# Rewritten first attention stage, early attention weights, late weights and a three-pass last stage in a program of eight stages

## The chip, the core and the metric

The program runs on one NeuronCore of one Trainium2 chip. The metric is the device time of one execution in microseconds (us), the median over the runs shown. PE is TensorE, ACT is ScalarE, DVE is VectorE, POOL is GpSimd and SP is SyncE, which here only issues DMAs. PSUM is the memory that PE writes its products to, in eight banks of 512 f32 columns; SBUF is the memory of the weights and the activations.

## What is computed

The input x is (8, 256, 256) in f32: eight items of 256 rows and 256 features. Eight stages follow each other, and each ends with the same step, x = layernorm(x + stage(x)):

- l0a: RMS norm, a projection to 1284 columns (gate 512, input 512, step 4, B and C 128 each), a causal convolution of 4 taps, SiLU, and a Mamba-2 scan with 4 heads and a state of 128
- l0f: gated MLP of 1024 with int8 weights
- l1a: attention with 16 heads of 128 (weights 256 x 6144 and 2048 x 256)
- l1f: mixture of 32 experts, 4 for each row
- l2a: Mamba-1 scan; l2f: gated MLP with ternary weights
- l3a: a transformer block with one key/value head, causal, and an MLP of 1024
- l3f: gated MLP of 688 with a shared LoRA and 8 LoRA experts of rank 8, 2 for each row

The heart of l0a, and l3f, cut to what matters:

```python
h = x * rsqrt(mean(x * x) + 1e-6) * norm_scale
proj = h @ in_proj_w                      # gate | ssm_in | dt_raw | B | C
ssm_in = silu(conv4(ssm_in) + conv_bias)
dt = softplus(dt_raw + dt_bias);  A = -exp(A_log)
cum = cumsum(A * dt)                      # within chunks; chained over them
y = (exp(cum_i - cum_j) * (C_i . B_j) * dt_j, only j <= i) @ x_h
y = (y + D * ssm_in) * silu(gate)
stage = x + y @ out_proj_w
```

```python
scores = sigmoid(x @ W_router); pick 2 of scores + expert_bias
gate = x @ W_gate + lora(x, sA_gate, sB_gate) + expert_lora(x, A_gate, B_gate, w)
up   = x @ W_up + ...                     # the same form
hidden = silu(gate) * up
out  = hidden @ W_down + ...              # the same form, on hidden
```

## The kernel before

The list `PHASES` holds one function for each stage, and the program calls them one after the other. x stays in SBUF throughout (`sh.X`). Each stage is a block with its own buffers, its own semaphores and one hand-written instruction stream for each engine; at its end all engines meet in a barrier. Nothing of a stage starts in the one before it. Within a stage all engines loop over the eight items, two per pass of a hardware loop (`Fori`); an item is two tiles of 128 rows. The order within an engine is the order of the code, and waits on semaphore counts tie the engines together. There is no planner.

**Before l0a** a first block loads all eight items of x.

**l0a.** SP loads eight small arrays, then the input weights wi and the output weights wo (L240 to L247), and PE's first projection (`project_in`, L293) waits for both. For each item: DVE scales the input rows (`scaled`, L463), PE turns them (L104), ACT keeps the result as xT (L112). `project_in` gives the input columns and the raw steps; DVE convolves (`convolve`, L479 and L481, 16 instructions), ACT takes SiLU (L395), PE turns the rows back. The decays are summed over runs and chunks (`sum_decays`), PE spreads the running sums over all partitions (cum) and turns the shares (L349); `share` is copied by DVE. Then come 16 instructions of DVE that add the share and the causal mask `hide` to the sums (ld, L589), the exponentials on ACT (lt, L433, L437, L441: two whole tiles of 512 columns and eight of 64), the products with CB and dt on DVE (mt, L599), the product with x on PE (yv), and on DVE yu (L608) and the gated yg (L613). PE turns yg and multiplies with wo (L380) into the bank Y. `add_and_stats` (L135) and `normalize` (L163) on DVE, with the square root between them on POOL (`rstd`, L156), end the item. The gates are projected into the same banks as the sums (W[4], W[5]), so they come first in an item and ACT takes their SiLU before the sums are written.

**l0f, l1a: three passes.** Here a product of two f32 matrices is three products of fp32r matrices (`product`, L787 and the lines behind it): high x high, low x high and high x low. ACT copies a matrix into its high half, DVE subtracts it from the original and leaves the low half. l0f's items have nine steps; DVE forms a (L759) and al, the low half of an earlier step's a (L765), and ACT the high half ah (L731). The down projection of an item (`down`, L684) waits for all eight al. In l1a SP loads the weights in 16 pieces into three slots; ACT casts (L966) and DVE subtracts (L1022) all 16 ahead of the first item, in their code, and PE waits for four pieces before every fourth head of the first item.

**l3a, l3f.** Each loads its weights at its own start (L2555 and following; L3072 and following). In l3a POOL makes wkr, a copy of the key weights (L2589), ahead of PE's first query product (L2629). l3f works in plain f32: per item five chunks of 128 hidden columns and one of 48, each with six products into one of three banks GU (L3119, L3120), the down projection with 24 instructions over 328 columns (L3131), then the LoRA end (haw turned, L3137 and L3141). `route` (L3180 to L3199) picks the experts on DVE, for the next item, behind the fourth chunk.

## Time and profile before

| | |
|---|---|
| Median of 3 runs (lowest, highest) | 2817.87 us (2817.5, 2819.13) |
| Profiled execution, its own time | 2824.52 us |
| Its span | 2822.8 us |
| PE busy (share) | 2324.8 us (82%) |
| DVE busy | 1728.7 us (61%) |
| ACT busy | 1424.7 us (50%) |
| POOL busy | 787.0 us (28%) |
| Granted clock of PE, mean | 0.902 of 2.4 GHz |

The stages stand in the span at: l0a 10.4 to 321.8 us, l0f to 455.2, l1a to about 1000, l1f to about 1540, l2a to 1988.5, l2f to 2143.4, l3a to 2555, l3f to 2814.1. Busy times are shares of the whole span, in which stages with different limits stand side by side; so windows by stage are read first, then the timeline of the engines within a stage. In a timeline a row gives the start, the duration, engine, line, operation, destination and sources, and in brackets how long the engine was idle before it and what released it; a row with xN stands for N instructions in succession.

### The profile page before, as it was taken

How to read it: one execution, taken by the hardware profiler on the slowest of the kernel's cores; microseconds unless marked ns; L12 is line 12 of the kernel's file. 1: busy time of each engine (PE TensorE's matmuls, PEld its weight loads, DVE VectorE, ACT ScalarE, POOL GpSimd, SP SyncE). 2: the span in 40 equal slices, each digit the busy share in tenths (PEclk: the TensorE clock that was granted, in tenths of full speed). 3: DMA queues.
4: the chain of work that ended last, by engine and by line, in shares of the span. 5: the costliest groups of instructions: out<-in, count | busy, mean ns of one | idle time of the engine just before them, and what ended most of it. 6: DMA issues, size and time to landing. Idle time of an engine off the chain costs nothing. (4 is left out here: it accounts for less than half of the span.)

```text
span 2822.8 us, 47695 instructions
## 1 busy us (share of the span) xinstructions
PE 2324.8 (82%) x15564; PEld 1976.3 (70%) x15564; DVE 1728.7 (61%) x4180; ACT 1424.7 (50%) x3573; POOL 787.0 (28%) x795
## 2 busy tenths in 40 slices
PE   4888783999999953999658888998685899895997
PEld 3666683999999952999536666777684567674765
DVE  4777575788888834554248888778463575641332
ACT  3444443777777711333267666775332665651222
POOL 1111010000000044000247787778483122220000
PEclk8777897999999956999879999999896999997999
DMA  4000003000000084333311111100001000001000
GB/s 123 0 0 0 14 0 119 1 2 2 3 2 3 2 247 135 116 117 102 115 57 46 46 46 46 57 35 1 23 0 42 1 1 0 0 0 43 0 0 30
DMA packets 77709, 111.40 MB, mean 39 GB/s; under 512 B 15162, under 2 KB 64050, under 8 KB 76484
## 3 DMA queue, kind: packets, MB, share of 16 engines
q1 hardware_dynamic: 70020, 87.36, 9.8%
q0 software_dynamic: 7488, 21.50, 2.4%
q8 instruction: 109, 1.79, 0.3%
q14 instruction: 92, 0.75, 0.1%
HBM read 79.86 MB, written 28.97 MB: 39 GB/s over the span
## 5 line engine op out<-in xcount | busy, mean ns | idle before, releaser
L1756 POOL TENSOR_TENSOR l2a_hb<-l2a_hb,l2a_Cb 128x1024 f32<-128x1024 f32 x128 | 303.2, 2380 | 112.8 <-DVE l2a_hb L2212 111.8
L2212 DVE TENSOR_TENSOR_SCAN l2a_hb<-l2a_dA,l2a_dB 128x1024 f32<-128x1024 f32 x128 | 288.4, 2274 | 63.0 <-PE l2a_dB L1837 30.1
L2066 ACT ACTIVATE l2a_dA<-l2a_delta,l2a_An 128x255 f32<-128x255 f32 x512 | 214.4, 497 | 37.2 <-DVE l2a_delta L2152 20.9
L1837 PE MATMUL l2a_dB<-l2a_diag,l2a_dxT 64*128 64x128 f32 x2048 | 190.9, 308 | 31.1 <-DVE l2a_hb L2212 18.3
L1837 PEld LDWEIGHTS l2a_dB<-l2a_diag,l2a_dxT 64*128 64x128 f32 x2048 | 141.5, 196 | 95.4 <-PE l2a_dB L1837 37.5
L793 PE MATMUL l1a_QK<-l1a_xh,l1a_wqkv_h 128*128 128x256 f32 x512 | 146.7, 286 | 13.7 <-DVE l1a_wo L1022 10.4
L793 PE MATMUL l1a_QK<-l1a_xh,l1a_wqkv 128*128 128x256 f32 x512 | 145.6, 284 | 0.0
L793 PE MATMUL l1a_QK<-l1a_xl,l1a_wqkv_h 128*128 128x256 f32 x512 | 145.4, 284 | 0.0
L1857 PE MATMUL l2a_YS<-ident,l2a_hb 128*128 128x128 f32 x1024 | 143.3, 287 | 1.0 <-POOL l2a_hb L1756 1.0
L1001 ACT ACTIVATE l1a_ex<-l1a_S,l1a_nm 128x256 f32<-128x256 f32 x256 | 119.2, 471 | 36.9 <-DVE l1a_nm L1053 36.9
L1857 PEld LDWEIGHTS l2a_YS<-ident,l2a_hb 128*128 128x128 f32 x1024 | 117.4, 146 | 12.4 <-issue 1.7
L2848 ACT ACTIVATE l3a_ex<-l3a_sm,l3a_nm 128x128 f32<-128x128 f32 (+1 forms) x256 | 99.0, 448 | 50.8 <-DVE l3a_nm L2985 50.2
L1036 DVE TENSOR_TENSOR l1a_qkl<-l1a_QK,l1a_qkh 128x512 fp32r<-128x512 f32 x128 | 88.2, 690 | 50.5 <-ACT l1a_qkh L976 37.1
L154 POOL TENSOR_TENSOR l1a_vpe<-l1a_mv,eps 128x2 f32<-128x2 f32 x8 | 1.6, 197 | 413.3 <-DVE l1a_mv L148 413.3
L1563 DVE TENSOR_TENSOR l1f_a<-l1f_s,l1f_GU 128x96 f32<-128x96 f32 x95 | 24.1, 254 | 143.3 <-ACT l1f_s L1417 143.3
L793 PEld LDWEIGHTS l1a_QK<-l1a_xh,l1a_wqkv_h 128*128 128x128 f32 x512 | 98.2, 192 | 14.4 <-issue 14.4
L2979 DVE TENSOR_TENSOR l3a_sm<-l3a_S,l3a_hide 128x512 f32<-128x512 f32 x96 | 65.7, 684 | 54.7 <-PE l3a_S L2698 54.7
L793 PEld LDWEIGHTS l1a_QK<-l1a_xl,l1a_wqkv_h 128*128 128x128 f32 x512 | 98.4, 192 | 0.0
L1353 PE MATMUL l1f_GU<-l1f_wS,l1f_xt 128*128 x380 | 98.3, 382 | 0.0
L793 PEld LDWEIGHTS l1a_QK<-l1a_xh,l1a_wqkv 128*128 128x128 f32 x512 | 98.3, 192 | 0.0
L976 ACT CAST l1a_qkh<-l1a_QK 128x512 fp32r<-128x512 f32 x128 | 75.6, 592 | 32.7 <-PE l1a_QK L793 32.4
L793 PE MATMUL l1a_S<-l1a_qkh 128*128 128x256 f32 x256 | 73.2, 286 | 22.4 <-DVE l1a_qkl L1036 22.2
(577 smaller groups left out, 7281.6 us busy)
## 6 DMA issues: line engine op xcount, KB each, us to landing
l2a_Cb<-c_rows SPq DMA_DIRECT2D x8, 2048.0 KB
l1f_xl<-moe_x_rows SPq DMA_DIRECT2D x95, 128.0 KB, 2.0
moe_y_rows<-l1f_yo SPq DMA_DIRECT2D x95, 128.0 KB, 1.7
l1a_raw<-in_L_attn_w_qkv_dram SPq DMA_DIRECT2D x12, 512.0 KB, 4.6
moe_x_rows<-X SPq DMA_DIRECT2D x1, 4224.0 KB, 17.3
l1f_dL<-in_L_ffn_Wd_dram SPq DMA_DIRECT2D x1, 3072.0 KB
X<-in_L_attn_x_dram SPq DMA_DIRECT2D x8, 256.0 KB, 4.6
l1a_raw<-in_L_attn_w_o_dram SPq DMA_DIRECT2D x4, 512.0 KB, 4.3
```

The source lines that it names most:

```text
L793: ins = pe.matmul(out, a, b, start=(first and n == 0), stop=(last and n == len(passes) - 1), **more)
L976: nc.scalar.copy(qkh[:, h % 2].rearrange("p n t -> p (n t)"), QK[h % 2][:, :]).then_inc(qk_kept, 1)
L1001: last = nc.scalar.activation(ex[:, h % 2, j, :], S[h % 2][:, j * SEQ:(j + 1) * SEQ], ACT.Exp, bias=nm[:, h % 2, j:j + 1], scale=SCALE, ac ...
L1036: nc.vector.tensor_tensor(qkl[:, h % 2].rearrange("p n t -> p (n t)"), QK[h % 2][:, :], qkh[:, h % 2].rearrange("p n t -> p (n t)").bitcas ...
L1353: last = nc.tensor.matmul(GU[t % 2][:, 2 * EI:2 * (EI + SI)], xt[t % 2][:, kc, :], wS[:, kc, bass.ds(small, 1), :], start=(kc == 0), stop= ...
L1756: nc.gpsimd.tensor_tensor(h[:, :, :], h[:, :, :], Cb[p][:, s0:s0 + UN, :], ALU.mult).then_inc(hc_ready, 1)
L1837: last = nc.tensor.matmul(out[:, m:m + 2, j * P + a:j * P + a + HP], dxT[q][a:a + HP, j, c * P:(c + 1) * P], diag[q][a:a + HP, j, s0 + m:s ...
L1857: last = nc.tensor.matmul(YS[j][:, c * P:(c + 1) * P], hb[u % RING][:, n, j * P:(j + 1) * P], sh.ident[:, :], is_transpose=True, start=Fal ...
L2066: last = nc.scalar.activation(dA[(i * NU + u) % DAS][:, n, 1:SEQ], delta[q][:, c, 1:SEQ], ACT.Exp, scale=An[:, c, s0 + n:s0 + n + 1])
L2212: nc.vector.tensor_tensor_scan(flat(hb[u % RING]), flat(dA[(i * NU + u) % DAS]), dB[u % 2][:, :], 0.0, ALU.mult, ALU.add).then_inc(scanned, 1)
L2848: last = nc.scalar.activation(ex[:, b % NB, cols], sm[:, b % NB, cols], ACT.Exp, bias=nm[:, b % NB, n:n + 1])
L2979: nc.vector.tensor_tensor(m, S[b % 3][:, :].rearrange("p (h k) -> p h k", h=nh), hide[:, None, 2 * P - keys_n:2 * P].to_broadcast([P, nh, ...
```

## The change

It has five parts.

1. **Loads at the start.** Only item 0 of x is loaded ahead of l0a. The other seven are issued in l0a by SP, behind wi and six of its small arrays, and before wo. The norm scale is loaded as two columns for each partition and applied by ACT when it keeps xT.
2. **l0a is rewritten.** The mask is added on PE: a bf16 identity times four copies of the mask, accumulated onto the sums in PSUM. ACT takes all exponentials straight from PSUM, 24 of 64 columns, with the share as bias; ld and its DVE instructions are gone. The gates go to the banks T and Y, late in an item. The projections, the convolution (now in two halves) and the decay sums of the next item are placed between the parts of the present one; what belongs to item i+1 or i+2 is left out in the last items by `left`. Items 0, 1, 6 and 7 are written out, 2 to 5 loop. The scaling of the input moves from DVE to ACT.
3. **Early weights.** l1a's wqkv is loaded, cast and subtracted in l0f, in 24 pieces of 512 columns, four in each of items 2 to 7. l1a itself keeps four pieces of wo, in steps 3 to 6 of its first item.
4. **Late weights.** The loads of l3a (23 DMAs) and l3f (21) are issued in l2f, behind its own, into buffers that stay until the end.
5. **l3f in three passes.** Weights, inputs, hidden tile and LoRA halves are split into high and low, and PE uses `product`. The end of an item (haw, LoRA, residual, normalisation) is moved behind the first chunks of the next.

The loads at the start, in SP's code of l0a:

```diff
-            sp.dma_start(nsb[:, :], row(w["L0_attn_norm_scale"])).then_inc(small_loaded, 16)
-            sp.dma_start(cw[:, :, :], w["L0_attn_conv_weight"]).then_inc(small_loaded, 16)
-            sp.dma_start(cb[:, :], w["L0_attn_conv_bias"]).then_inc(small_loaded, 16)
+            sp.dma_start(ns[:, :], w["L0_attn_norm_scale"]).then_inc(ns_loaded, 16)
+            sp.dma_start(wi[:, :, :], w["L0_attn_in_proj_w"].rearrange("(k p) n -> p k n", p=P)).then_inc(w_loaded, 16)
...
+            sp.dma_start(cw[:, :, :], w["L0_attn_conv_weight"]).then_inc(small_loaded, 16)
+            sp.dma_start(cb[:, :], w["L0_attn_conv_bias"]).then_inc(small_loaded, 16)
+            for b in range(1, ITEMS):
+                sp.dma_start(sh.X[:, b], sh.x_dram[:, b]).then_inc(sh.x_rest, 16)
             sp.dma_start(Db[:, :], row(w["L0_attn_D"])).then_inc(small_loaded, 16)
-            sp.dma_start(wi[:, :, :], w["L0_attn_in_proj_w"].rearrange("(k p) n -> p k n", p=P)).then_inc(w_loaded, 16)
             sp.dma_start(wo[:, :, :], w["L0_attn_out_proj_w"].rearrange("(k p) n -> p k n", p=P)).then_inc(w_loaded, 16)
```

PE in one item of l0a (after the inputs are turned), and the mask:

```diff
                 last.then_inc(la_turned, 1)
 
+            def mask(j):
+
+                return nc.tensor.matmul(W[4 + j][:, :], identb[:, :], hide4[:, :, :].rearrange("p h t -> p (h t)"),
+                                        start=False, stop=True, skip_group_check=True)
+
+            def decays(k):
+
+                pe.wait_ge(yT_kept, k * NT)
+                pe.wait_ge(cumR_ready, (k + 1) * 2)
+                for j in (1, 0):
+                    for h in range(NH):
+                        last = nc.tensor.matmul(W[4 + j][:, h * P:(h + 1) * P], sel[:, h, :], cumR[:, j * P:(j + 1) * P],
+                                                start=(h == 0), stop=(h == NH - 1), skip_group_check=True)
+                    if j == 0:
+                        last = mask(0)
+                    last.then_inc(cum_ready, 1)
+                pe.wait_ge(share_ready, k + 1)
+                for n in range(len(SHARES)):
+                    last = nc.tensor.matmul(W[3][:, SEQ + n * NH:SEQ + (n + 1) * NH], shareR[:, n, :], ph.ident[0:NH, 0:NH],
+                                            start=True, stop=True)
+                last.then_inc(share_turned, 1)
...
+                if left:
+                    steps_in(i + 1, 1 - p)
+                    pe.wait_ge(xtm_ready, (i + 1) * NT)
+                    ssm_in(i + 1, 1 - p, 0)
+                pe.wait_ge(lt_ready, i * 3 + 1)
+                mask(1).then_inc(mask_ready, 1)
+                if left:
+                    ssm_in(i + 1, 1 - p, 1)
+                pe.wait_ge(ph.y_added, i)
+                for j, bank in enumerate((ph.T, ph.Y)):
+                    for kc in range(KC):
+                        last = nc.tensor.matmul(bank[:, :], ph.xT[p][:, kc, j * P:(j + 1) * P], wi[:, kc, 0:DI],
+                                                start=(kc == 0), stop=(kc == KC - 1))
+                    last.then_inc(gate_ready, 1)
+                pe.wait_ge(xtm_ready, (i + 1) * NT)
```

ACT's exponentials in an item of l0a:

```diff
+                    nc.scalar.copy(xtm[p][:, j, :], W[j][:, :]).then_inc(xtm_ready, 1)
+                act.wait_ge(m_ready, i * 3)
+                act.wait_ge(share_kept, i + 1)
+                act.wait_ge(cum_ready, (i + 1) * NT)
+                for n in ORDER:
+                    s, t = BLOCKS[n]
+                    if n == 2:
+                        act.wait_ge(mask_ready, i + 1)
                     for h in range(NH):
                         for u in range(NT):
-                            last = nc.scalar.activation(lt[:, 1, h, u * CHUNK:(u + 1) * CHUNK],
-                                                        W[5][:, h * P + u * CHUNK:h * P + (u + 1) * CHUNK], ACT.Exp,
-                                                        bias=share[:, SHARES.index((0, NT + u)), h:h + 1])
+                            cols = slice(u * CHUNK, (u + 1) * CHUNK)
+                            m = SHARES.index((s, NT * t + u))
+                            last = nc.scalar.activation(lt[:, n, h, cols], W[4 + t][:, h * P + u * CHUNK:h * P + (u + 1) * CHUNK],
+                                                        ACT.Exp, bias=share[:, m, h:h + 1])
                     last.then_inc(lt_ready, 1)
-                    nc.scalar.activation(lt[:, 2], ld[:, 1], ACT.Exp).then_inc(lt_ready, 1)
+                if left:
```

DVE in the same item:

```diff
+                    steps.begin(i + 1)
+                    dt_magnitude(i + 1)
+                dve.wait_ge(cb_ready, i + 1)
+                dve.wait_ge(yv_ready, i * NT)
+                for done, n in enumerate(ORDER):
+                    s, t = BLOCKS[n]
+                    dve.wait_ge(lt_ready, i * 3 + done + 1)
+                    for h in range(NH):
+                        last = nc.vector.scalar_tensor_tensor(out=mt[:, n, h, :], in0=W[2][:, n * P:(n + 1) * P],
+                                                              scalar=dt[:, s, h:h + 1], in1=lt[:, n, h, :],
+                                                              op0=ALU.mult, op1=ALU.mult)
+                    last.then_inc(m_ready, 1)
+                if left:
+                    one_plus(i + 1)
+                    convolve(i + 1, (0, 1))
+                for j in range(NT):
```

The early pieces in l0f, on SP, ACT and DVE, and those that stay in l1a, on DVE:

```diff
+            for m in range(PIECES):
+                if m >= SLOTS:
+                    sp.wait_ge(early.low_ready, m - SLOTS + 1)
+                kc, c = m // (PIECES // KC), m % (PIECES // KC) * 512
+                sp.dma_start(raw[m % SLOTS][:, :].bitcast(F32), early.src[:, kc, c:c + 512]).then_inc(qkv_loaded[m % SLOTS], 16)
...
+                    if 4 <= step < 4 + SLOTS and split:
+                        act.wait_ge(qkv_loaded[step - 4], (i - 1) * 16)
+                        nc.scalar.copy(high[:, i * 4 - 8 + step - 4, :], raw[step - 4][:, :].bitcast(F32)).then_inc(early.high_ready, 1)
...
+                    if 5 <= step < 5 + SLOTS and split:
+                        n = i * 4 - 8 + step - 5
+                        dve.wait_ge(early.high_ready, n + 1)
+                        nc.vector.tensor_tensor(low[:, n, :], raw[step - 5][:, :].bitcast(F32), high[:, n, :].bitcast(F32),
+                                                ALU.subtract).then_inc(early.low_ready, 1)
...
+                        dve.wait_ge(w_high, step - 2)
+                        _, came, high, low = piece(step - 3)
+                        nc.vector.tensor_tensor(low, came, high.bitcast(F32), ALU.subtract).then_inc(w_low, 1)
```

The late loads, in l2f:

```diff
+            sh.late.load_l3_attn(sp)
+            sh.late.load_l3_ffn(sp)
```

l3f: a chunk and the down projection on PE, the hidden tile's high half on ACT and low half on DVE:

```diff
+                    for half, wh, wl, bh, bl in ((0, wgh, wgl, bgh, bgl), (1, wuh, wul, buh, bul)):
+                        parts = [(wh[:, kc, cols], wl[:, kc, cols], xh[p][:, kc, :], xl[p][:, kc, :]) for kc in range(KC)]
+                        parts += [(bh[:, cols], bl[:, cols], xawh[:, p, half, :], xawl[:, p, half, :])]
+                        last = product(nc.tensor, GU[n % 3][0:rows, half * SEQ:(half + 1) * SEQ], parts)
...
+                        router_and_a(pe, i + 1, 1 - p)
+                pe.wait_ge(ph.y_added, i * NT)
+                if first:
+                    pe.wait_ge(w_low, 6)
+                for j in range(NT):
+                    tile = slice(j * P, (j + 1) * P)
+                    for f, rows in CH:
+                        if j == 0:
+                            pe.wait_ge(hid_low, i * FC + f + 1)
+                        if j == 0 and f == FC - 1:
+                            turn_xaw(pe, i + 1)
+                        last = product(nc.tensor, YB[j][:, 0:D + LR],
+                                       [(hh[0:rows, f, tile], hl[0:rows, f, tile], wdh[0:rows, f, :], wdl[0:rows, f, :])],
+                                       first=(f == 0), last=(f == FC - 1))
...
+                        act.wait_ge(gu_used, i * FC + f + 1)
+                        if f == 0:
+                            act.wait_ge(down_ready, i * NT)
+                        nc.scalar.copy(hh[0:rows, f, :], hid[0:rows, n % 3, :]).then_inc(hid_high, 1)
...
+                        dve.wait_ge(hid_high, i * FC + f + 1)
+                        nc.vector.tensor_tensor(hl[0:rows, f, :], hid[0:rows, n % 3, :], hh[0:rows, f, :].bitcast(F32), ALU.subtract
+                                                ).then_inc(hid_low, 1)
```

How the change moves instructions is shown at three places. The first is ACT in l0a, in the order of the code before: xT is kept, then the exponentials of the decays (lt, from the tiles ld and from the bank W) and the SiLU of the next item's convolution (xs from cv).

```order
L112 COPY l0a_xT<-l0a_T 128x512
L431 REGISTER_ALU
L433 ACT_TABLE_LOAD
L433 ACTIVATE l0a_lt<-l0a_ld 128x512
L437 ACTIVATE l0a_lt<-l0a_W,l0a_share 128x64 x8
L441 ACTIVATE l0a_lt<-l0a_ld 128x512
L392 REGISTER_ALU
L394 ISA
L395 ACT_TABLE_LOAD
L395 ACTIVATE l0a_xs<-l0a_cv,l0a_cb 128x256
```

With the change, from keeping xT to the end of the gates (sg):

```order
L456 ACTIVATE l0a_xT<-l0a_T,l0a_ns 128x256 x2
L489 COPY l0a_xtm<-l0a_W 128x512 x2
L501 ACT_TABLE_LOAD
L501 ACTIVATE l0a_lt<-l0a_W,l0a_share 128x64 x24
L470 ACTIVATE l0a_e<-l0a_ax 128x8
L474 ACT_TABLE_LOAD
L474 ACTIVATE l0a_ln<-l0a_w 128x8
L510 ACT_TABLE_LOAD
L510 ACTIVATE l0a_sg<-l0a_T 128x512
L510 ACTIVATE l0a_sg<-l0a_Y 128x512
```

The exponentials are 24 small instructions now, all from PSUM; the exponential of the step (e) follows them directly, and the gates' SiLU stands behind them and not ahead.

The second place is DVE in the loop of l0f, before: a, its low half al, and the normalisation of the item before (L163).

```order
L759 SCALAR_TENSOR_TENSOR l0f_a<-l0f_GU,l0f_su,l0f_gs 128x256
L765 TENSOR_TENSOR l0f_al<-l0f_a,l0f_ah 128x256
L756 REGISTER_ALU
L759 SCALAR_TENSOR_TENSOR l0f_a<-l0f_GU,l0f_su,l0f_gs 128x256
L765 TENSOR_TENSOR l0f_al<-l0f_a,l0f_ah 128x256
L163 TENSOR_SCALAR X<-l0f_r,l0f_mv,l0f_rstd 128x256
```

And with the change:

```order
L862 SCALAR_TENSOR_TENSOR l0f_a<-l0f_GU,l0f_su,l0f_gs 128x256
L868 TENSOR_TENSOR l0f_al<-l0f_a,l0f_ah 128x256
L878 ISA
L879 ISA
L879 TENSOR_TENSOR early_wqkv<-l0f_raw,early_wqkv_h 128x512
L859 REGISTER_ALU
L862 SCALAR_TENSOR_TENSOR l0f_a<-l0f_GU,l0f_su,l0f_gs 128x256
L868 TENSOR_TENSOR l0f_al<-l0f_a,l0f_ah 128x256
L163 TENSOR_SCALAR X<-l0f_r,l0f_mv,l0f_rstd 128x256
```

A difference of 128x512 elements stands behind al in each of the steps 5 to 8 of an item.

The third is PE in l3f, the first product of a chunk, before:

```order
L3119 MATMUL l3f_GU<-l3f_xT,l3f_wg 128x256 x2
L3120 MATMUL l3f_GU<-l3f_xawT,l3f_bg 128x256
L3119 MATMUL l3f_GU<-l3f_xT,l3f_wu 128x256 x2
L3120 MATMUL l3f_GU<-l3f_xawT,l3f_bu 128x256
L3119 MATMUL l3f_GU<-l3f_xT,l3f_wg 128x256 x2
```

With the change, the half of a chunk that makes the gate:

```order
L901 MATMUL l3f_GU<-l3f_xh,l3f_wgh 128x256
L901 MATMUL l3f_GU<-l3f_xl,l3f_wgh 128x256
L901 MATMUL l3f_GU<-l3f_xh,l3f_wgl 128x256
L901 MATMUL l3f_GU<-l3f_xh,l3f_wgh 128x256
L901 MATMUL l3f_GU<-l3f_xl,l3f_wgh 128x256
L901 MATMUL l3f_GU<-l3f_xh,l3f_wgl 128x256
L901 MATMUL l3f_GU<-l3f_xawh,l3f_bgh 128x256
L901 MATMUL l3f_GU<-l3f_xawl,l3f_bgh 128x256
L901 MATMUL l3f_GU<-l3f_xawh,l3f_bgl 128x256
```

Each f32 product has become three.

## Rows read from the trace of the kernel before

**Rows 1.** Windows: us, busy (count) of PE, PEld, DVE, ACT, POOL; clock, DMA, GB/s

```profile
10.40:321.80 311.40, 232.94 (x1126) 192.57 (x1126) 208.94 (x680) 141.61 (x282) 36.36 (x49) 0.80 0.07 21
455.20:512.00 56.80, 21.92 (x140) 20.93 (x140) 30.66 (x44) 29.35 (x49) 1.68 (x4) 0.64 0.47 148
512.00:1000.00 488.00, 478.60 (x3994) 476.77 (x3992) 396.80 (x1071) 375.74 (x1129) 12.36 (x23) 1.00 0.01 2
1988.50:2143.40 154.90, 117.83 (x884) 113.68 (x884) 87.61 (x220) 53.56 (x143) 104.65 (x158) 0.87 0.03 11
2555.00:2814.10 259.10, 219.25 (x960) 161.75 (x960) 70.89 (x325) 59.65 (x104) 12.31 (x27) 0.93 0.05 12
```

**Rows 2.** Timeline of the start: start, us, engine, line, operation, count, [idle before <-releaser]

```profile
14.68 0.47 SPq L247 DMA_DIRECT2D l0a_wo<-n_L_attn_out_proj_w_dram  x1
...
23.82 0.79 PE L293 MATMUL l0a_W<-l0a_xT,l0a_wi 128*128 128x256 f32 x1 [2.47 <-DMA l0a_wo<-n_L_attn_out_proj_w_dram]
```

**Rows 3.** Timeline of one item of l0a

```profile
152.20 2.77 DVE L463 SCALAR_TENSOR_TENSOR l0a_xin<-X,l0a_inv,l0a_nsb 128x256 f32<-128x256 f32 x2 [0.92 <-POOL l0a_inv L255]
...
158.06 1.28 ACT L433 ACT_TABLE_LOAD   x1 [0.38 <-DVE l0a_ld L589]
...
159.89 1.73 ACT L437 ACTIVATE l0a_lt<-l0a_W,l0a_share 128x64 f32<-128x64 f32 x8
...
160.01 1.12 DVE L599 SCALAR_TENSOR_TENSOR l0a_mt<-l0a_W,l0a_dt,l0a_lt 128x128 f32<-128x128 f32 x4 [0.50 <-ACT l0a_lt L433]
...
165.41 5.02 DVE L481 SCALAR_TENSOR_TENSOR l0a_cv<-l0a_W,l0a_cw,l0a_cv 128x255 f32<-128x255 f32 x12
...
181.61 0.69 DVE L135 SCALAR_TENSOR_TENSOR l0a_r<-X,l0a_Y 128x512 f32<-128x512 f32 x1 [2.01 <-PE l0a_Y L380]
...
184.44 0.74 DVE L163 TENSOR_SCALAR X<-l0a_r,l0a_mv,l0a_rstd 128x256 f32 x2 [1.08 <-POOL l0a_rstd L156]
```

**Rows 4.** Line L613: count, min/median/max ns, first and last start

```profile
L613 DVE TENSOR_TENSOR l0a_yg<-l0a_yu,l0a_sg x16: 680/681/685, 69.5 to 308.9; 128x512 f32<-128x512 f32 x16
```

**Rows 5.** Window of l0f's steady part, and DVE's timeline in it

```profile
340.00:440.00 100.00, 90.05 (x725) 86.20 (x724) 71.96 (x187) 49.87 (x125) 11.78 (x18) 1.00 0.00 1
...
357.72 1.02 DVE L163 TENSOR_SCALAR X<-l0f_r,l0f_mv,l0f_rstd 128x256 f32<-128x256 f32 x2
...
394.67 0.68 DVE L126 TENSOR_TENSOR l0f_xl<-l0f_T,l0f_xh 128x512 fp32r<-128x512 f32 x1
...
442.67 0.73 DVE L163 TENSOR_SCALAR X<-l0f_r,l0f_mv,l0f_rstd 128x256 f32 x2
```

**Rows 6.** Timeline of l1a's start, ACT, DVE and PE

```profile
459.02 0.69 DVE L126 TENSOR_TENSOR l1a_xl<-l1a_T,l1a_xh 128x512 fp32r<-128x512 f32 x1 [3.95 <-ACT l1a_xh L119]
...
460.11 1.04 ACT L966 CAST l1a_wqkv_h<-l1a_raw 128x1024 fp32r<-128x1024 f32 x1 [1.12 <-DMA l1a_raw<-in_L_attn_w_qkv_dram]
...
461.18 1.23 DVE L1022 TENSOR_TENSOR l1a_wqkv<-l1a_raw,l1a_wqkv_h 128x1024 fp32r<-128x1024 f32 x1 [1.47 <-ACT l1a_wqkv_h L966]
...
495.97 0.58 PE L793 MATMUL l1a_S<-l1a_qkh 128*128 128x256 f32 x1 [22.23 <-DVE l1a_qkl L1036]
```

**Rows 7.** Timeline of l3a's start, the first query matmuls on PE

```profile
2164.71 1.62 PE L2629 MATMUL l3a_T<-l3a_xT,l3a_wq 128*128 128x256 f32 x3 [16.23 <-POOL l3a_wkr L2589]
```

**Rows 8.** Timeline of PE in l3f, and a window of 40 us in l1a

```profile
2581.98 2.07 PE L3119 MATMUL l3f_GU<-l3f_xT,l3f_wg 128*128 128x256 f32 x4 [0.75 <-ACT l3f_xawT L3152]
...
2640.52 1.03 PE L3119 MATMUL l3f_GU<-l3f_xT,l3f_wg 128*128 128x256 f32 x4
...
2641.39 0.60 PE L3120 MATMUL l3f_GU<-l3f_xawT,l3f_bg 72*128 72x256 f32 x2
...
2658.86 7.47 PE L3131 MATMUL l3f_Y<-l3f_wd,l3f_hid 128*128 128x328 f32 x24 [0.99 <-DVE l3f_hid L3217]
...
2668.80 1.03 PE L3119 MATMUL l3f_GU<-l3f_xT,l3f_wg 128*128 128x256 f32 x4
...
520.00:560.00 40.00, 40.00 (x338) 40.00 (x337) 32.04 (x85) 31.98 (x96) 0.84 (x1) 1.00 0.01 2
```

848 lines of the change are left out of this document (484 added, 364 removed).

## The prediction

> **What bounds the kernel now.** I read the busy time by stage first. The change touches the stages l0a (first attention), l0f, l1a, the start of l2f, l3a and l3f [rows 1]. TensorE (PE) is the busiest engine in each, but only l1a behind its first 57 us is solid: 478.60 us busy in 488.00. In l0a PE is busy for 232.94 of 311.40 us and is granted a clock of 0.80 on average (1 is 2.4 GHz, 0.50 is 1.2 GHz); l1a's first part has 21.92 busy in 56.80.
>
> Then the timeline, for what ends PE's waits. At the start the output weights are issued at 14.68 us, behind the input weights, and the first projection runs at 23.82, released by them [rows 2]. In l0a the reader is to see a serial chain over DVE, ACT and PE [rows 3, 4]. In l1a PE's second group of work starts at 495.97 after 22.23 us of waiting, behind casts of 1.04 us (ACT) and differences of 1.23 us (DVE) that turn the weights into two halves [rows 6]. l3a waits 16.23 us for weights [rows 7], and l3f starts only at 2581.98 and then runs in f32 at about 0.216 us per instruction, two instructions per product [rows 8].
>
> **The change, part by part.** Its own time is 2824.52 us for a span of 2822.8; the median of the runs is 2817.87. I take the difference of spans off the median.
>
> *Start and l0a.* Only one of eight input tiles is loaded ahead of the stage; seven move behind the projection weights, but the output weights stand behind all of these, and PE waits for both. Behind the stage's start, which comes some 7 us earlier, the loads carry 4.0 MB instead of 2.2. I put the first projection at 19 us; bounds are 17 (all moves at the rate of a full queue) and 24 (as now). From 19 on: projections at the low clock and two taps of the convolution 9.7; dt, la and the sums 4.7; the other taps 3.4; silu, staging, turn and copies 4.8, which is 41.6; from the table load to the first gated product 12.8 as in the cycle below, and 0.8 for slow matmuls: 55.2. That product (L613) now starts at 69.5 [rows 4]: 14.3 less.
>
> A cycle runs from one item's gated products to the next; there are two an item, 0.6 apart, so it is (308.9-69.5-0.6)/7 = 34.1 us [rows 4]. The new one, at PE's full clock: DVE forms dt and la (0.95), PE turns la (0.65), DVE sums (2.9), convolves two taps (8 of the 12 instructions of 5.02 us: 3.35), then 0.2, and the residual chain from 181.61 to 185.18 (3.57) [rows 3], and copies the shares (0.25): 11.9. ACT loads its table (1.28) and takes 24 exponentials at 1.73/8 = 0.216: 5.2, with gaps 6.65. This makes 18.55. DVE multiplies the last block (1.12), forms 1+e (0.4), convolves two taps (3.3), and adds and gates (1.28 each): 26.2 with a few gaps. Gone from it are DVE's 16 additions of mask and share, each of 64 columns, now two bf16 matmuls of 512 columns on PE, for which no row stands (twice fp32r's 0.118 for 256 columns is 0.24 each [rows 8]), two table loads, and the scaled input on DVE, 2.77 us beside POOL's product [rows 3]. The later stages of PE, behind the share copy, are 11.2 us of matmuls, and reach the same point as DVE, 23.7 against 23.5: no slack. A clock of 0.9 adds 1.2 us. I take 27.5. The bounds are 26.2, and 31, which is 29.1 us (232.94/8) of PE busy time as now plus 2 of waits. Six cycles give 6 x 6.6 = 39.6. The last cycle has no next item to prepare: 24.5 against 34.1, 9.6 less. The tail, from the last gated pair to the stage's end at 321.7, falls from 13.4 to 8.1, since the sums for a next item no longer stand in it: 5.3. Sum **-68.8**.
>
> *l0f.* Items 2 to 7 take four pieces of the l1a weights each, a cast on ACT and a two-input difference of 128x512 on DVE. DVE is busy for 71.96 of 100 us and ACT for 49.87 [rows 5], so by averages it all fits. But the down projection waits for DVE's last difference (al), and three of the four new ones stand ahead of it in DVE's queue. An instruction of this size takes 0.68 [rows 5]: 6 items x 3 x 0.69 = 12.4, and I take **+13**; the bounds are 0 (hidden by the waits that DVE has) and 20 (4 each, and PE's clock falling once an item). The pair of normalisations takes 1.02 us beside POOL's copy of an input tile and 0.73 in the item where there is none [rows 5]. The Trainium skill (SBUF — State Buffer, Who interferes with whom) says that a DVE instruction with two SBUF inputs and a GpSimd instruction that reads SBUF exclude each other for a whole instruction; by it each item might lose another POOL copy's length, and the term would be nearer to its upper bound. That speaks against the pieces being placed here.
>
> *l1a.* Weights are ready, so the first group of S products can follow at 464 us instead of 495.97: the input's low half is ready at 459.7, two halves of QK at the 1.2 GHz level take 2.5, the split 1.2. Four pieces of wo stay, in the first item's steps 3 to 6, 1.04 and 1.23 each beside a DVE that is 80% busy (396.80 of 488.00): they cost 1.5 [rows 1, 6]. **-30.5**, bounds -24 (the pieces delay their full length) and -33.
>
> *l2f.* 44 loads are issued behind the three that its start waits for. **+0.5**, bounds 0 and 4 (they share the engines with these three). The issue time itself, 44 x 0.47 = 21 us, lies beside 150 us of the stage.
>
> *l3a.* PE has turned the input when its 16.23 us of waiting begin, at 2148.5 [rows 7]; ACT keeps it in 1 us more, POOL's copy of the key weights (0.4) is done before that, so the first query matmul runs at 2149.7 instead of 2164.71: **-15**, bounds -13 and -16.
>
> *l3f.* Weights are there; ACT and DVE split four of them first, 4.2 and 5.0 us by the elements of [rows 6], behind the routing: start at 2570.7, 11.3 less. An f32 product of 256 columns costs two instructions of 0.216; three fp32r passes cost 3 x 0.118, as 40 us of l1a hold 338 of them [rows 8]. So GU falls from 15.5 to 12.7 us an item. The down projection has 328 columns: now 24 instructions in 7.47 us; 36 passes of 0.118 x 328/256 = 0.15 make 5.4 (bounds 4.9 and 6.2: the f32 form needs 10% over its share). With turns, router and the LoRA end PE has 20.9 us. The LoRA end of an item is moved behind the next item's first chunk, so that chain leaves the path, but a new one enters: scores wait for ACT behind chunk 3, routing takes 3.3 us of DVE, and the fifth and sixth differences come behind it, while PE stands at the down projection. I get 2.6 us of waits: 23.5 an item, against 28.3 (2668.80-2640.52, [rows 8]). Eight items with 3.5 of slow clock at first: 191.5, against 228.3 now (2640.52-2581.98 for the first two, and six more). The tail is 2 longer. **-46.1**, bounds -34 and -54.
>
> Sum: -68.8+13-30.5+0.5-15-46.1 = -146.9. 2817.87-146.9 = **2671**.
>
> **The rivals.** *The clock follows the small waits.* The two rewritten stages wait briefly and often. l2f does so with 117.83 busy in 154.90 and is granted 0.87; but l0f's steady part runs at 1.00 and l3f at 0.93, its start included [rows 1, 5]. With l2f's clock, 20.9 becomes 24.0 in l3f, +25 us; in l0a the cycle goes to 29.6, +15: 2711. The Trainium skill (TensorE: Matmul & The Clock Gate, A second HAM failure mode: psum-queue depth-cycling) has it that short, frequent idling between matmul groups that cycle through PSUM banks makes the clock oscillate; l3f's three banks would fit that, and the granted 1.00 of l0f's steady part, which cycles through four, speaks against it [rows 5].
>
> *DVE and ACT set l3f's cycle.* The hidden tile now needs six casts and six differences more and two hand-overs per chunk. If the routing chain costs 7 us and not 2.6, the item is back at 28 us and only the start is gained: 2671+36 = 2707. For it speaks that the order of each engine is fixed; against, that DVE is busy for 70.89 of 259.10 us there now [rows 1].
>
> *The loads don't hide.* Early pieces late, or l2f's first loads slowed: 2690.
>
> *Slower.* In both rewritten stages PE's clock stays at the 1.2 GHz level throughout. Then l0a's 22.4 us of matmuls become 45 a cycle, +76-14 = +62, and l3f's items 42, +110-9 = +101; with l0f +13 and -45.5 from l1a and l3a this gives 2949. It decides once the mean clock of both falls below some 0.62; l0a now has 0.80 with longer waits than I expect, which speaks against it.
>
> **How the numbers follow.** Forecast 0.75, clock rival 0.12, l3f's cycle 0.08, loads 0.03, slower 0.02. The first has its own range from its bounds, added as independent: 2650 to 2695. To keep 8 in 10 with the two rivals near 2710, the range is 2645 to 2712. A measurement here tells 0.2% (5.6 us) from no change; only the last case is on the other side, and 0.01 is left to no change: faster 0.97, same 0.01, slower 0.02.
>
> **What would show it.** In the trace of the changed kernel: first projection near 19 us; gated products 27.5 us apart; l0f's items 16.3 us apart instead of 14.2 ((442.67-357.72)/6, [rows 5]), with PE waiting for al; l1a's first S product 8 us behind its start; no DMA wait in l3a; fp32r at 0.118 in l3f, a wait of some 1.6 us in the down projection, 23.5 us an item, clock 0.9 or more. An l0a clock under 0.8, or an l3f item over 26, would make the prediction wrong.

## The result, and the profile after

The changed kernel takes 2675.48 us (median of 4 runs, 2671.42 to 2687.0) against 2818.5 us for the kernel before (4 runs): the ratio is 0.9493, with an interval of 0.9466 to 0.9521. That is 143.0 us less; 146.9 less was forecast, and 2671. The profiled execution is the longest of the four, 2687.0 us of its own time for a span of 2685.3; what follows is read from it. Further down, one run of the kernel before (3229.18 us, at a granted clock of 0.713) is a slow one and left out of its median and its ratios.

The page of the changed kernel, busy time by engine, and PE's granted clock in 40 slices:

```profile
PE 2271.4 (85%) x15926; PEld 1964.0 (73%) x15926; DVE 1702.8 (63%) x4081; ACT 1443.0 (54%) x3765; POOL 781.0 (29%) x796
...
PEclk9888999999999758999779989999797999998999
```

PE is busy for 53.4 us less than before and the span is 137.5 us shorter, so most of the gain is waiting that is gone. A stage is taken here from the end of the last normalisation (L163) of the stage before to the end of its own last one:

| stage, us | before | after | difference | forecast |
|---|---|---|---|---|
| start and l0a | 321.7 | 258.5 | -63.2 | -68.8 |
| l0f | 133.4 | 141.8 | +8.4 | +13 |
| l1a | 544.8 | 508.5 | -36.3 | -30.5 |
| l1f to l2f | 1143.4 | 1150.4 | +7.0 | +0.5 |
| l3a | 411.6 | 397.2 | -14.4 | -15 |
| l3f | 258.9 | 219.7 | -39.2 | -46.1 |

The +7.0 is no effect of the change. 6.5 of it lie in the expert loop of l1f, which the change does not touch: from its first to its last matmul it took 264.8 us before and 271.3 here. Among the twelve experiments below, all with this loop, eleven take 264.8 to 266.1 and one 273.0 (`g_three`), and the stretch from l1f to l2f takes 1129.4 to 1144.2 us. So the loop takes one of two lengths with the same code; why is open. It may also be what sets the profiled execution 11 us above the median; the other runs have no trace that would show it.

Windows of the changed kernel (us, busy and count of PE, PEld, DVE, ACT and POOL; clock, DMA share, GB/s): l0a's steady part, l0f's, the start of l1a, l2f, and l3f:

```profile
100.00:208.00 108.00, 103.98 (x545) 85.50 (x545) 75.20 (x248) 68.10 (x199) 14.31 (x20) 0.88 0.00 1
300.00:380.00 80.00, 66.13 (x534) 63.07 (x533) 61.48 (x157) 43.82 (x108) 8.44 (x15) 1.00 0.22 66
400.50:457.30 56.80, 48.90 (x371) 46.99 (x372) 38.88 (x92) 39.01 (x107) 2.28 (x5) 0.91 0.12 38
1905.00:2059.00 154.00, 116.59 (x884) 112.07 (x884) 87.66 (x224) 53.52 (x143) 105.06 (x159) 0.88 0.17 49
2456.00:2676.00 220.00, 191.47 (x1344) 176.30 (x1344) 101.96 (x399) 81.29 (x164) 12.33 (x27) 0.93 0.00 1
```

l0a's steady part has become one in which PE is busy for 96% of the time. Before, the steady part had 82%, in the next line (75% in [rows 1] is with the start):

```profile
100.00:300.00 200.00, 163.13 (x798) 135.68 (x799) 143.11 (x470) 98.77 (x198) 25.27 (x30) 0.80 0.00 0
```

l1a's first 57 us hold 48.90 us of PE where they held 21.92; l2f, with 17% of DMA beside it, is as long as it was. l0f went the other way: 83% of PE where it had 90% [rows 5].

The two gated products an item in l0a (count, min/median/max ns, first and last start), to be set beside [rows 4]:

```profile
L674 DVE TENSOR_TENSOR l0a_yg<-l0a_yu,l0a_sg x16: 681/683/686, 58.3 to 249.7; 128x512 f32<-128x512 f32 x16
```

A cycle is (249.7-58.3-0.6)/7 = 27.3 us.

The timeline of the changed kernel at the places that the forecast named (start, duration, engine, line, operation, idle before it and releaser):

```profile
21.44 1.87 PE L311 MATMUL l0a_W<-l0a_wi,l0a_xT 128*128 128x4 f32 x8 [11.52 <-DMA l0a_wo<-n_L_attn_out_proj_w_dram]
...
174.87 1.86 PE L365 MATMUL l0a_W<-ident,l0a_shareR 4*128 4x4 f32 x12
...
222.48 1.28 DVE L674 TENSOR_TENSOR l0a_yg<-l0a_yu,l0a_sg 128x512 f32<-128x512 f32 x2
...
249.10 1.28 DVE L674 TENSOR_TENSOR l0a_yg<-l0a_yu,l0a_sg 128x512 f32<-128x512 f32 x2
...
337.38 0.69 DVE L133 TENSOR_TENSOR l0f_r<-X,l0f_ys 128x512 f32<-128x512 f32 x1
...
344.24 0.38 PE L784 MATMUL l0f_Y<-l0f_wd,l0f_ah 128*128 128x256 f32 x1 [1.59 <-DVE l0f_al L868]
...
352.61 0.69 DVE L133 TENSOR_TENSOR l0f_r<-X,l0f_ys 128x512 f32<-128x512 f32 x1
...
405.08 0.55 PE L901 MATMUL l1a_QK<-l1a_xh,early_wqkv_h 128*128 128x256 f32 x1 [1.49 <-DVE l1a_xl L126]
...
409.38 0.39 PE L901 MATMUL l1a_S<-l1a_qkh 128*128 128x256 f32 x1
...
2065.64 1.62 PE L2712 MATMUL l3a_T<-l3a_xT,late_wq 128*128 128x256 f32 x3 [1.27 <-ACT l3a_xT L2890]
...
2473.34 0.55 PE L901 MATMUL l3f_GU<-l3f_xh,l3f_wgh 128*128 128x256 f32 x1 [4.19 <-DVE l3f_xawl L3341]
...
2542.53 0.52 DVE L3329 TENSOR_TENSOR l3f_xaw<-l3f_LX,l3f_wf 128x144 f32<-128x144 f32 x2
...
2543.31 0.41 DVE L3367 TENSOR_TENSOR l3f_hl<-l3f_hid,l3f_hh 128x256 fp32r<-128x256 f32 x1
...
2543.78 0.42 PE L901 MATMUL l3f_Y<-l3f_wdh,l3f_hh 128*128 128x328 f32 x1 [1.32 <-DVE l3f_hl L3367]
...
2545.61 0.60 PE L3176 MATMUL l3f_XT<-ident,l3f_xaw 128*72 128x128 f32 x4 [0.46 <-DVE l3f_hl L3367]
```

What is to be seen, in order of time. The first projection is still released by the output weights, which stand behind seven input tiles now; PE has waited 11.52 us for them. In l0f an item is 352.61-337.38 = 15.23 us long (14.15 before, from [rows 5]), and the down projection waits for al, as the forecast had it. Over five items PE's wait for al is 1.62 us in the mean, against 0.19 before. l1a's first S product starts at 409.38, 9.1 us behind the stage's start at 400.3; it had been 40.9. l3a has no DMA wait left: the query product waits only for its input, 6.4 us behind the start at 2059.2 (21.4 before). And in l3f the low half hl, on which the down projection waits, comes right behind the end of the routing chain (L3329) in DVE's order.

### The profile page after: what moved, and what is told of

Its sections match the earlier page's. It is cut to its first block and busy times, and to the rows that moved or that the text cites. A ratio compares the mean times of both kernels' runs of the same rounds, so it can differ in the third digit from the quotient of the medians.

```text
span 2685.3 us, 48369 instructions
## 1 busy us (share of the span) xinstructions
PE 2271.4 (85%) x15926; PEld 1964.0 (73%) x15926; DVE 1702.8 (63%) x4081; ACT 1443.0 (54%) x3765; POOL 781.0 (29%) x796
## 5 line engine op out<-in xcount | busy, mean ns | idle before, releaser
L2314 DVE TENSOR_TENSOR_SCAN l2a_hb<-l2a_dA,l2a_dB 128x1024 f32<-128x1024 f32 x128 | 288.4, 2275 | 62.5 <-PE l2a_dB L1939 28.8
L2168 ACT ACTIVATE l2a_dA<-l2a_delta,l2a_An 128x255 f32<-128x255 f32 x512 | 214.3, 497 | 37.5 <-DVE l2a_delta L2254 20.9
L1939 PEld LDWEIGHTS l2a_dB<-l2a_diag,l2a_dxT 64*128 64x128 f32 x2048 | 141.8, 197 | 96.3 <-PE l2a_dB L1939 37.8
L901 PE MATMUL l1a_QK<-l1a_xh,early_wqkv_h 128*128 128x256 f32 x512 | 144.2, 282 | 5.1 <-issue 3.6
L901 PE MATMUL l1a_QK<-l1a_xl,early_wqkv_h 128*128 128x256 f32 x512 | 143.2, 280 | 0.0
L901 PE MATMUL l1a_QK<-l1a_xh,early_wqkv 128*128 128x256 f32 x512 | 143.1, 280 | 0.0
L1665 DVE TENSOR_TENSOR l1f_a<-l1f_s,l1f_GU 128x96 f32<-128x96 f32 x95 | 24.1, 254 | 140.0 <-ACT l1f_s L1519 140.0
L901 PEld LDWEIGHTS l1a_QK<-l1a_xh,early_wqkv_h 128*128 128x128 f32 x512 | 97.3, 190 | 5.9 <-issue 5.9
L901 PEld LDWEIGHTS l1a_QK<-l1a_xl,early_wqkv_h 128*128 128x128 f32 x512 | 97.2, 190 | 0.0
L901 PEld LDWEIGHTS l1a_QK<-l1a_xh,early_wqkv 128*128 128x128 f32 x512 | 97.1, 190 | 0.0
L2938 ACT COPY l3a_eT<-l3a_PT 128x512 f32<-128x512 f32 x96 | 55.4, 577 | 70.9 <-PE l3a_PT L2827 70.8
L1091 ACT ACTIVATE l1a_pr<-l1a_ex,l1a_rz 128x256 f32<-128x256 f32 x128 | 65.3, 510 | 44.0 <-DVE l1a_rz L1142 40.4
```

The source lines that it names most:

```text
L901: ins = pe.matmul(out, a, b, start=(first and n == 0), stop=(last and n == len(passes) - 1), **more)
L1091: nc.scalar.activation(pr0[:, h % 2, :], ex[:, h % 2, 0, :], ACT.Copy, scale=rz[:, h % 2, 0:1]).then_inc(probs_ready, 1)
L1939: last = nc.tensor.matmul(out[:, m:m + 2, j * P + a:j * P + a + HP], dxT[q][a:a + HP, j, c * P:(c + 1) * P], diag[q][a:a + HP, j, s0 + m:s ...
L2168: last = nc.scalar.activation(dA[(i * NU + u) % DAS][:, n, 1:SEQ], delta[q][:, c, 1:SEQ], ACT.Exp, scale=An[:, c, s0 + n:s0 + n + 1])
L2314: nc.vector.tensor_tensor_scan(flat(hb[u % RING]), flat(dA[(i * NU + u) % DAS]), dB[u % 2][:, :], 0.0, ALU.mult, ALU.add).then_inc(scanned, 1)
```

## The experiments

The first four kernels undo one part each; they ran on one chip, where the kernel before took 2813.09 us (7 runs). The change itself did not run beside these or the later kernels. Its 2675 us go with 1150.4 us from l1f to l2f, and these four take 1129.4 to 1135.2 there; so their totals come out below the expected ones, and the reading goes by stage. A stage with unchanged code is not the same in every profile either: l0a takes 255.0 to 258.5 us, l3f 216.5 to 222.9.

### The old l0a

The stage and its first loads are those of before; the rest is changed.

```diff
-            for b in range(1, ITEMS):
-                sp.dma_start(sh.X[:, b], sh.x_dram[:, b]).then_inc(sh.x_rest, 16)
...
-                mask(1).then_inc(mask_ready, 1)
...
+                    nc.scalar.activation(lt[:, 0], ld[:, 0], ACT.Exp).then_inc(lt_ready, 1)
```

> The changed kernel with the first attention stage and the first loads of before (all eight input tiles ahead of the stage). Parts add up: l0a ends at 321.7 us again and not at 258.5, nothing behind it moves, 2675 + 63 = 2739 us. Parts depend on each other (the early pieces or the stage behind profit from what l0a leaves, a clock or a queue): the other stages change their length and the sum is off by more than 5 us from 2739.

Measured: 2726.89 us, ratio 0.970 (0.9678 to 0.9722). l0a is back at 320.4 us, +61.9 against the change, and l0f, l1a, l3a and l3f stay within 1.6 us of it. The total is 12 us below the expected 2739, which by its own words speaks for parts that depend on each other. But the stretch from l1f to l2f, at 1131.3 us, is 19 us shorter than in the change's profile, and it is as short (1129.4 to 1135.2) in the three kernels beside it that keep the new l0a. So the stages do not lean on each other, and the terms can be read one by one.

### The old weights of l1a

l0f has no pieces, and l1a loads and splits all 16 of its own.

```diff
-                    item(it * 2 + p, p, split=True)
+                    item(it * 2 + p, p)
...
+            for m in range(len(PIECES)):
+                dve.wait_ge(w_high, m + 1)
+                _, came, high, low = piece(m)
+                nc.vector.tensor_tensor(low, came, high.bitcast(F32), ALU.subtract).then_inc(w_low, 1)
```

> The changed kernel with l0f and l1a of before: all 16 weight pieces are split in front of l1a's first item. If the pieces cost l0f their displacement of al and the missing split is l1a's whole gain: l0f's items go from 15.27 back to 14.1-14.2 us, the stage from 141.8 to 133-134, l1a from 508.5 to 545; 2675 + 28 = 2703 us. Rival: l0f is longer for another reason (its start behind the new l0a); then it stays above 140 us and the time is 2711.

Measured: 2701.33 us, ratio 0.9594 (0.9566 to 0.9622). l0f takes 134.0 us (-7.8), l1a 547.9 (+39.4). The part is worth 31.6 us by its stages and would be worth 39 if l0f paid nothing. l0f's items are back at 14.1 us, so the new l0a ahead of it is not what made them longer.

### The late loads in their own stages

The same DMAs, issued at the start of l3a and of l3f.

```diff
-            sh.late.load_l3_attn(sp)
-            sh.late.load_l3_ffn(sp)
...
+        @block.sync
+        def _(sp):
+            sh.late.load_l3_attn(sp)
```

> The changed kernel with the 23 and 21 late loads issued at the starts of l3a and l3f themselves. If they are hidden in l2f: l2f keeps 154 us; l3a gets its wait of about 14.5 us back; in l3f the router product runs 19 us behind the stage's start instead of 4.2, 15 us more; 2675 + 29 = 2704 us. Rival: the 44 loads and their buffers cost something in l1f, l2a or l2f (the three were 7 us longer in the profile of the change): then these three return to 1143 us together and the time is 2697.

Measured: 2686.21 us, ratio 0.9548 (0.9522 to 0.9574). l3a is some 11 us longer than this change's in the other kernels (408.3 against 396.6 to 397.6), l3f 13.0 longer (232.7 against 219.7), both somewhat less than expected, and l1f to l2f take 1129.4 us against 1129.7, 1131.3 and 1135.2 in its neighbours on the chip: the 44 transfers cost l2f nothing that can be seen.

### l3f in f32

The changed l3f with its order and its early weights, but one f32 product where there are three of fp32r. The low halves are formed and not used.

```diff
-        xh, xl = ([ph.sb(f"{n}{q}", [P, KC, SEQ], F32R) for q in range(2)] for n in ("xh", "xl"))
+        xh, xl = ([ph.sb(f"{n}{q}", [P, KC, SEQ], F32) for q in range(2)] for n in ("xh", "xl"))
...
-                        last = product(nc.tensor, GU[n % 3][0:rows, half * SEQ:(half + 1) * SEQ], parts)
+                        last = single(nc.tensor, GU[n % 3][0:rows, half * SEQ:(half + 1) * SEQ], parts)
```

> The changed kernel with l3f in its new order but in f32: one f32 product where three fp32r ones stand; the casts and differences stay (the low halves are then zero and no product reads them). If the gain is in PE's passes: an item goes from 24.3 to 27.5-29 us (GU +2.8, down +2.1, less a wait of 1.5), 2675 + 26 to 38, about 2707 us. Rival: the new order of the item is what gained: the item stays under 26 us and the time under 2689.

Measured: 2682.95 us, ratio 0.9537 (0.9514 to 0.9561); l3f takes 236.0 us, +16.3. Its window of 140 us:

```profile
2500.00:2640.00 140.00, 138.94 (x615) 101.90 (x614) 57.78 (x234) 44.99 (x96) 7.22 (x15) 1.00 0.00 0
```

And the same window of the changed kernel:

```profile
2500.00:2640.00 140.00, 131.44 (x943) 122.50 (x941) 64.87 (x268) 51.60 (x111) 8.65 (x18) 0.96 0.00 1
```

In f32 PE is busy for 99% of it and an item takes 26.6 us; with three passes PE is busy for 94% and an item takes 24.1 to 24.35 (one took 28.4, at a lower granted clock). So the shorter products free more of PE than the stage gets. The outcome lies between the two expectations: an item is shorter than the 27.5 to 29 us of the first and longer than the 26 of its rival, since the new order is worth something too. With one f32 product, PE's busy time in an item is as before (26.5 us against 26.6), and its waits fall from 1.66 us to 0.1: from 28.3 to 26.6 an item, 13 us in eight. Of the whole 39.2 us of l3f, then, 13.0 are the loads and 16.3 the three passes; 9.9 are left for the order less what the splitting at the start costs, and these two were not taken apart.

### Four parts moved alone

These ran together on another chip (kernel before 2812.22 us, 3 runs), two runs each. The first brings l3f's routing forward by a step, behind the second chunk, and sets the residual behind it:

```diff
-                    if step == 2 and not first:
-                        residual(i - 1)
-                    if step == 3:
+                    if step == 2:
                         route(dve, i + 1, 1 - p)
+                    if step == 3 and not first:
+                        residual(i - 1)
```

> The changed kernel; in l3f router, scores and routing of the next item come one chunk earlier (router behind chunk 1, scores and routing in step 2, the residual in step 3). If the down projection waits because the routing stands ahead of the last differences on DVE: its waits (2.4 us an item) go to under 0.5, PE's clock rises above 0.96, an item takes 21.5-22.3 us instead of 24.3 and l3f 199-206 us instead of 219.7. Rival: the wait only moves (chunk 3's hidden tile now waits for the routing): an item stays above 23.5 us and l3f above 213.

Measured: 2663.17 us, ratio 0.9475 (0.9432 to 0.9518). l3f takes 217.0 us, where kernels with the change's l3f took 216.5 to 222.9, so nothing is won: an ordinary item takes 24.6 us, even 0.5 more than in the change. This is the rival of the expectation. PE's waits in one item, from its timeline:

```profile
2543.45 0.42 PE L901 MATMUL l3f_Y<-l3f_wdh,l3f_hh 128*128 128x328 f32 x1 [0.90 <-DVE l3f_r L3349]
...
2547.33 0.60 PE L3176 MATMUL l3f_XT<-ident,l3f_xaw 128*72 128x128 f32 x4 [0.74 <-DVE l3f_hl L3367]
```

The routing chain is gone from the place ahead of the down projection, and the residual is what PE waits for in its stead. The wait of 1.32 and 0.46 became one of 0.90 and 0.74.

The second forms the four differences of an item of l0f behind its last al, not between the al:

```diff
-                    if 5 <= step < 5 + SLOTS and split:
-                        n = i * 4 - 8 + step - 5
+                    if step == FC and split:
+                        for m in range(SLOTS):
+                            n = i * 4 - 8 + m
```

> The changed kernel; in l0f the four early differences of an item stand together behind its last al, and no longer between the steps. If they cost by standing ahead of al: PE's wait for al (about 1.6 us an item) goes to under 0.4, an item takes 14.1-14.5 us instead of 15.27 and l0f 134-137 us instead of 141.8. Rival: DVE has no room behind al either (a of the next item comes 2.4 us later): the item stays at 15 us or more.

Measured: 2660.66 us, ratio 0.9466 (0.9425 to 0.9508). Two residuals in its timeline, to be set beside 337.38 and 352.61 above:

```profile
332.67 0.69 DVE L133 TENSOR_TENSOR l0f_r<-X,l0f_ys 128x512 f32<-128x512 f32 x1
346.76 0.69 DVE L133 TENSOR_TENSOR l0f_r<-X,l0f_ys 128x512 f32<-128x512 f32 x1
```

The item is back at 14.1 us, PE's wait for al at 0.19, and l0f at 134.4: DVE does the same work, and none of it stands ahead of something that PE waits for. The place, and not the amount, was the price.

The third raises l0a's clock: six bf16 products of 512 columns an item, whose result nobody reads, in place of the idling around the small products of the shares.

```diff
+            def filler():
+
+                nc.tensor.matmul(W[2][:, :], identb[:, :], hide4[:, :, :].rearrange("p h t -> p (h t)"), start=True, stop=True)
...
+                for _ in range(3):
+                    filler()
```

> The changed kernel; in l0a six bf16 products of 512 columns into a free bank (their result is overwritten unread) stand between and behind the share products, 0.21 us each at full clock, 1.3 us an item. If it is the run of tiny products (12 instructions with 4 columns) and the short wait behind them that brings PE's clock down to the 1.2 GHz level for 5 us an item: the mean clock from 100 to 208 us rises from 0.88 to 0.97 or more, and an item takes 24.3-25 us instead of 26.05 although PE does more. Rival: the clock falls for another reason: it stays under 0.92 and an item takes 26.8-27.4 us.

Measured: 2668.68 us, ratio 0.9495 (0.9461 to 0.9528). Its window of l0a:

```profile
100.00:208.00 108.00, 102.69 (x553) 80.73 (x560) 74.38 (x242) 68.88 (x199) 15.37 (x18) 0.94 0.00 1
```

The clock goes from 0.88 to 0.94, which is less than expected, and the stage is not shorter: 261.3 us against 258.5, and against 255.0 and 257.0 in the two kernels beside it that have the change's l0a. The products of 256 columns (L319) take 384 ns in the mean where they took 476. Part of what they save goes to the fillers themselves, some 1.3 us an item, and part to new waits, as the timeline shows:

```profile
159.70 1.89 PE L319 MATMUL l0a_W<-l0a_xT,l0a_wi 128*128 128x256 f32 x8 [1.01 <-ACT l0a_lt L510]
```

The fourth lets the first projections wait for the input weights alone. The output weights get a semaphore of their own, PE waits for it ahead of their first product, and the squares of the second item are taken later.

```diff
-            sp.dma_start(wo[:, :, :], w["L0_attn_out_proj_w"].rearrange("(k p) n -> p k n", p=P)).then_inc(w_loaded, 16)
+            sp.dma_start(wo[:, :, :], w["L0_attn_out_proj_w"].rearrange("(k p) n -> p k n", p=P)).then_inc(wo_loaded, 16)
...
-            pe.wait_ge(w_loaded, 32)
+            pe.wait_ge(w_loaded, 16)
...
+            pe.wait_ge(wo_loaded, 32)
```

> The changed kernel; in l0a PE's first projection waits for the input weights alone (the output weights have a count of their own, waited for ahead of the first item), and ACT squares item 1 behind item 0's step sizes. If the wait for the output weights, issued behind seven tiles of x, is what holds the start: the first projection runs at 11-13 us instead of 21.4, the first gated product 7 to 9 us earlier than 58.3, and l0a ends 7 to 9 us earlier. Rival: the small loads and x hold the chain: less than 3 us.

Measured: 2651.71 us, ratio 0.9434 (0.9401 to 0.9468). PE at its start:

```profile
11.10 1.84 PE L311 MATMUL l0a_W<-l0a_wi,l0a_xT 128*128 128x4 f32 x8 [1.19 <-ACT l0a_xT L457]
```

The first projection comes 10.3 us earlier than in the change's profile, the first gated product at 47.7 instead of 58.3, and l0a ends 11.0 us earlier, at 247.5. Against the two kernels beside it on the chip with the change's l0a (`e_diffs_last` and `e_early_route`: first projection at 19.94 and 20.02, end of l0a at 257.0 and 255.0), it is 8.9 us at the first projection and 7.5 to 9.5 at the end, within or near the 7 to 9 expected: nearly the whole of the start's wait was on the path.

### Putting them together

The times of the four kernels in this section are those of the edits at work, and none of the four is a kernel to take over: what they return is off from the right result by a relative 0.034, the same in all four. Each of the two edits that all four share, the own semaphore and the late differences, returns the right result by itself; why the two together do not is open. The expert loop has the same 380 matmuls of each kind in all of them as in the change.

The kernel before took 2821.59 us beside the next two (6 runs). The first takes four edits: the own semaphore, the late differences, a third order of DVE in l3f (residual right behind the hidden tile of step 2, then routing, normalisation behind the last difference), and in l0a the scaling of the input ahead of SiLU.

```diff
+                    if step == 2 and not first:
+                        residual(i - 1)
...
-                    if step == 3:
+                    if step == 2:
                         route(dve, i + 1, 1 - p)
-                    if step == 5 and not first:
+                    if step == FC and not first:
                         normalize(ph, dve, i - 1)
...
-                if left:
-                    silu_xs(i + 1)
                 if left > 1:
                     stage_scaled(act, i + 2)
+                if left:
+                    silu_xs(i + 1)
```

> Four edits, each in a stage of its own or in a part that no other touches: the start of l0a with the input weights alone and l0f with its differences behind the last al (both as measured before: l0a's start 10 us earlier, l0f 134.4 us); in l0a ACT scales the input of item i+2 ahead of item i+1's SiLU and DVE forms its mean square behind yg; in l3f router and routing one chunk earlier as before, but the residual right behind hid in step 2, where DVE waits for ACT, and the normalisation behind the last difference. If l0a's cycle is a chain over DVE, ACT and PE and not PE's clock: 1.2-1.5 us less a cycle (0.9 scaling, 0.2, 0.3 of waits), l0a 237-240 us. Rival for l0a: PE is the bound (96% busy): stays at 246-248. If l3f's wait follows what stands ahead of the last differences on DVE: item 22-22.8 us, l3f 203-209 us. Rival for l3f: the wait moves once more: l3f 214-218 us. Sum of the four by the theories: 2675 - 10.6 - 7.4 - 9 - 13 = 2635 us, and some 15 less on a chip on which the three untouched stages between l1a and l3a take 1130 us and not 1150.

Measured: 2641.0 us, ratio 0.936 (0.9334 to 0.9386). l3f is at 202.1 us; l0a, at 249.8, is no shorter than with the own semaphore alone (247.5), nor than in the two kernels below without the earlier scaling (245.6 and 246.6), so the earlier scaling gives nothing.

The second is the same with the fillers, and with the differences of l0f on POOL:

```diff
+                        pool.wait_ge(early.high_ready, n + 1)
+                        nc.gpsimd.tensor_tensor(low[:, n, :], raw[m][:, :].bitcast(F32), high[:, n, :].bitcast(F32),
+                                                ALU.subtract).then_inc(early.low_ready, 1)
```

> The four edits with two changes: the early differences of l0f on POOL instead of DVE, and the fillers between and behind the share products in l0a. POOL is busy for 14 of 142 us in l0f, so by busy time l0f ends at 133-135 us as with the differences behind al. Rival (DVE and POOL hold each other up over SBUF): DVE's two-input instructions (al 0.41 us, mt) get longer mean times, and l0f takes over 137 us; a difference on POOL takes 1.2 us or more. Fillers: if with the shorter chain PE is now the bound, the higher clock pays and l0a is 3 us or more below the kernel with four edits; if the chain still bounds, l0a is the same or longer.

Measured: 2682.9 us, ratio 0.9511 (0.9483 to 0.9539): 42 us slower than without these two edits, 35.3 of them in l0f (169.7 against 134.4; an item takes 20.6 us). l0a is 4.3 us longer in spite of a clock of 0.94. DVE's groups in l0f of this kernel (count, busy us, mean ns):

```profile
L884 DVE TENSOR_TENSOR l0f_al<-l0f_a,l0f_ah 128x256 fp32r<-128x256 f32 x39 | 24.5, 639 | 0.6 <-ACT l0f_ah L847 0.3
...
L163 DVE TENSOR_SCALAR X<-l0f_r,l0f_mv,l0f_rstd 128x256 f32 x10 | 13.1, 1354 | 0.0
```

The same two in the changed kernel:

```profile
L868 DVE TENSOR_TENSOR l0f_al<-l0f_a,l0f_ah 128x256 fp32r<-128x256 f32 x41 | 17.3, 422 | 0.5 <-ACT l0f_ah L831 0.3
...
L163 DVE TENSOR_SCALAR X<-l0f_r,l0f_mv,l0f_rstd 128x256 f32 x10 | 3.6, 403 | 0.0
```

And one item in the timeline, POOL, DVE and PE:

```profile
325.64 5.47 POOL L781 TENSOR_TENSOR early_wqkv<-l0f_raw,early_wqkv_h 128x512 f32 x4
...
325.96 2.63 DVE L163 TENSOR_SCALAR X<-l0f_r,l0f_mv,l0f_rstd 128x256 f32 x2
...
328.90 2.49 DVE L884 TENSOR_TENSOR l0f_al<-l0f_a,l0f_ah 128x256 fp32r<-128x256 f32 x2
...
331.06 0.80 POOL L94 COPY l0f_xin<-X 128x512 f32 x1
...
331.92 1.12 PE L104 MATMUL l0f_T<-ident,l0f_xin 128*128 128x128 f32 x4 [5.86 <-POOL l0f_xin L94]
```

Two things happen. The four differences stand in POOL's queue ahead of its copy of the next input tile, and PE waits 5.86 us for that copy, where it had waited 0.50; that is most of the item's 6.5 us. And in the 5.47 us in which POOL works, DVE's instructions last about three times as long, two normalisations 2.63 us and two differences 2.49. The Trainium skill (SBUF — State Buffer, Who interferes with whom) has a DVE instruction with two SBUF inputs and a GpSimd instruction that reads SBUF lock each other out of shared ports for a whole instruction, and the trace agrees for the difference al, 422 ns in the mean in the change and 639 here. The normalisation reads one tile only and is stretched all the same. That is so without this edit too: in l0f of the kernel before, the first of each pair runs beside a POOL instruction and takes 696 to 698 ns, the second has none beside it and takes 401 to 403. The runs do not tell how the loss divides between the two causes, since no kernel puts the pieces behind POOL's copy.

The last two leave the useless edit away (kernel before 2818.03 us, 9 runs; 5 runs of each). The first holds the own semaphore, the late differences and the third order of l3f; the second only the first two:

```diff
-                if left > 1:
-                    stage_scaled(act, i + 2)
                 if left:
                     silu_xs(i + 1)
+                if left > 1:
+                    stage_scaled(act, i + 2)
```

> The changed kernel with three edits: the first projection waits for the input weights alone; l0f's early differences behind the last al; in l3f routing one chunk earlier, with the residual behind hid in step 2 and the normalisation behind the last difference. l0a is as in the change but for the start. From the stages measured one by one: l0a 247.5, l0f 134.4, l1a 508.5, l3a 397.2, l3f 202 us, 9 at the end, and 1130 to 1150 us between (chip by chip): 2629 to 2649 us, a ratio to the kernel before of 0.936 to 0.939. If the stages lean on each other (the scaling moved in l0a gave l3f or l0f part of this), l3f is over 206 or l0f over 137 us.

```diff
+                    if step == 2 and not first:
+                        residual(i - 1)
+                    if step == 3:
...
+                    if step == 5 and not first:
                         normalize(ph, dve, i - 1)
```

> The same without the edit in l3f: l0a 247.5, l0f 134.4, l3f 217-220 us; 15 to 17 us more than the kernel with three edits, a ratio to the kernel before of 0.942 to 0.945.

Measured: 2641.91 us with the three, ratio 0.9373 (0.9354 to 0.9392), and 2656.91 with the two, 0.9427 (0.9411 to 0.9444): 15.0 us between them, as expected. The window of l3f with the three, and DVE's timeline in it:

```profile
2480.00:2600.00 120.00, 119.85 (x888) 111.69 (x887) 62.30 (x265) 48.67 (x104) 9.21 (x18) 1.00 0.00 0
```

```profile
2500.32 0.42 DVE L3363 TENSOR_TENSOR l3f_hid<-l3f_GU,l3f_gs 128x256 f32<-128x256 f32 x1 [3.11 <-ACT l3f_gs L3277]
2500.66 0.74 DVE L3351 TENSOR_TENSOR l3f_r<-X,l3f_Y 128x256 f32<-128x256 f32 x2
...
2502.40 0.39 DVE L3371 TENSOR_TENSOR l3f_hl<-l3f_hid,l3f_hh 128x256 fp32r<-128x256 f32 x1
```

PE waits for nothing at all, its clock is full, and an item takes 22.4 us; l3f takes 201.9 us in the profile, against 222.6 with two, which is at the long end of 216.5 to 222.9 since two of its items ran at a lower clock:

```profile
2535.00:2560.00 25.00, 24.99 (x157) 23.67 (x158) 7.98 (x35) 8.07 (x17) 1.44 (x3) 0.80 0.00 0
```

The residual now falls where DVE would have waited 3 us for the next gate anyway, and the normalisation behind everything that PE needs. Which of these two places did it, beside the early routing that alone did nothing, was not tried. PE busy by item is 26.4 us in f32 (26.6 x 138.94/140) and 22.4 here, so the three passes are worth 4.0 us an item, of which the change had kept 2.5 in an ordinary item (26.6 against 24.1).

## Why the prediction was right

The likeliest case came in, 4.5 us off, within its own range of 2650 to 2695. The mechanisms were the ones named; several sizes were not, and they partly cancelled. That the total is so near is in part luck: by stages, l0a and l3f gave 5.6 and 6.9 us less than forecast, l0f and l1a 4.6 and 5.8 more, and the profiled execution has 6.5 us more in the untouched loop.

- **Start and l0a (-68.8 forecast, -63.2 measured).** The step that was off is the first projection, put at 19 us; it came at 21.44, since its releaser stands behind seven tiles of 256 KB; 2.4 of the 5.6 us are there (in the experiments with the same loads it came at 19.9 to 20.2). The first gated product follows 36.9 behind it, where the sum had 36.2. The first six cycles take (222.48-58.31)/6 = 27.4 us where I had 27.5, with a clock of 0.88 where I had 0.9. The last takes 26.6 (249.10-222.48) and not 24.5, and the tail behind it 9.4 and not 8.1: having no next item to prepare was worth less than I took it for. "No slack" between PE and the chain over DVE and ACT fits the experiments but is not shown by them: a higher clock gives nothing (the fillers), the earlier scaling gives nothing, and the one kernel with both (`f_pool_fill`) gives nothing either. Over the same five cycles the mean is 27.6 us in the change, 27.9 with the fillers, 27.6 with the scaling, and 27.6 with both. The fillers cost PE time of their own, so the clock by itself was not tried. The start's wait, which I had taken as a given of the change, was worth 7.5 to 11 us by a semaphore.
- **l0f (+13, +8.4).** The place and the reason are right: putting the pieces last removes the cost. Three pieces of 0.69 ahead of the last al make 2.07 us an item, and 1.1 were paid (15.23 against 14.15). PE's waits show where: that for al went from 0.19 to 1.62 us, so 1.43 of the 2.07 reached PE, and that for the next input tile fell from 0.51 to 0.22. The further loss beside POOL's copy, with which the upper bound was argued, did not come: the normalisations no longer run beside that copy, and take 403 ns each where the first of a pair took 697. So the term that was mis-sized is the displacement, 12.4 forecast and 8.4 measured.
- **l1a (-30.5, -36.3).** The start gained 31.8 us (40.9 to 9.1 behind the stage's start), as forecast, if 8.9 is set beside 9.1. The pieces of wo were thought to cost 1.5 us; the rest of the stage is instead 4.5 us shorter (499.4 against 503.9). Why was not tried.
- **l2f (+0.5).** Nothing to be seen, by the kernel with the loads in their own stages.
- **l3a (-15, -14.4).** The first query product came 6.4 us behind the stage's start, 15.0 earlier than before.
- **l3f (-46.1, -39.2).** Start 16.9 us behind the stage's beginning where the sum had 15.8. The item, 23.5 in the sum, takes 24.1 to 24.35, and one of the eight 28.4. The chain behind the routing was put right as the place, at 2.6 us of waits; the trace shows 1.32 and 0.46 us of them in one item and 1.5 in the mean of three, so the waits are smaller than I had them and PE's own time is longer: 22.4 to 22.6 where I had 20.9. That is the term that was mis-sized.

Of the rivals, that of the clock came true in its picture and only in part in its price. l0a's clock does fall, to 0.88 in the mean. In one item it goes from 0.96 to 0.50 behind the twelve share products of four columns, as the windows of 2 us show.

```profile
174.00:176.00 2.00, 2.00 (x17) 1.65 (x15) 2.00 (x6) 1.71 (x4) 0.44 (x1) 0.96 0.00 0
176.00:178.00 2.00, 1.39 (x7) 1.31 (x8) 1.07 (x6) 1.00 (x3) 0.95 (x3) 0.50 0.00 0
...
184.00:186.00 2.00, 2.00 (x6) 1.55 (x6) 1.49 (x6) 1.47 (x8) 0.00 (x0) 0.50 0.00 0
```

It stays there for some 10 us, in the item before for some 4. The cycle is 27.4 us all the same, as forecast with a clock of 0.9; whether it would be shorter at the full clock was not shown by the fillers. In l3f the clock fell too, in one item of the change (28.4 us where the others take 24.1): six of the eight profiles with the change's order of l3f have one or two such items of 27.3 to 28.8 us, so each such fall costs up to 4.7 us. What sets it off is open. With waits of 0.90 and 0.74 us an item (the early routing) the clock was granted in full over the window of 140 us: short waits alone did not bring it down there. The Trainium skill (TensorE: Matmul & The Clock Gate, A second HAM failure mode: psum-queue depth-cycling) would have short idling between groups make the clock oscillate; the window of the early routing does not show it. DVE and ACT do not set l3f's cycle: once they are ordered by what PE waits for, they hide altogether. The slower case had nothing.

## What to carry to other kernels

Let a first product wait only for its own weights; a shared semaphore count silently adds whatever is queued behind them. Side work on a helper engine costs by its place in that engine's order: put it behind the last thing that the busiest engine waits for, and look for the helper's own waits to put it into. After PE's products get shorter, order the helpers anew, since the saving goes to waits first (2.5 of 4.0 us came through until then). When PE and a chain over the others look equally long, shortening one of them may show nothing, as here in l0a; that shortening both helps was not shown.

## What the runs showed of the hardware

- A difference of 128x512 takes 680 ns on DVE and 1397 ns in the mean on POOL, where it stretches DVE's instructions beside it: the normalisation of 128x256 from 403 to 1354 ns, though it has a single tile as its input. POOL's copy of an input tile stretches it to 697 ns.
- PE's busy share says little of its granted clock: 96% busy went with 0.88 (l0a), 94% with 0.96 and 99.9% with 1.00 (l3f). Before the falls in l0a PE ran products of 4 columns.
- An untouched loop (l1f's) took 264.8 to 266.1 us in twelve of the fourteen profiles, and 271.3 and 273.0 in the other two. A difference between two kernels of a few us is read by stage, not by the total.
